# Logits between projections and scores: another order on TensorE and VectorE in a fused attention and soft-mixture kernel

## The chip, the core and the metric

The kernel runs on one core of a Trainium2 chip. The metric is the device time of one execution in microseconds, from a program that computes everything in a single launch.

## The reference

For x of shape 16 x 256 x 128 (4096 tokens of width 128), layer-normalised to xn, three things are added up:

```python
out = x + attention(xn) + soft_moe(xn)
# attention: 2 x 16 heads of width 64, causal, o = softmax(q1 k1) v1 - lam * softmax(q2 k2) v2, then o @ Wo
# soft_moe:
logits = (xn @ phi_w.T + phi_b).reshape(t, z, 64, 32)     # 64 experts x 32 slots = 2048 columns
D = softmax(logits, axis=3)                               # over an expert's 32 slots: "dispatch"
C = softmax(logits, axis=2)                               # over the 64 experts: "combine"
X_tilde = einsum('tznp,tzd->npd', D, xn)                  # then clip, layernorm, tanh
Y = einsum('tznp,npH->tzH', C, X_tilde @ expert_w + expert_b)
```

Everything is in 32-bit floats. Most products are made of three matmuls (`product3`) from high and low halves of the operands.

## The kernel before

The kernel has three phases: setup (layer norm, transposes of xn), a main phase and a combine phase. The change is in the main phase alone.

The main phase walks through 128 steps, written as `for it in range(ITER + 2): for j in range(4): step(it, j, ...)`, with `ITER` = 32. A step v = 4 it + j does two things side by side.

* Attention for one sequence and four heads: two sequences of one group of heads are a unit, and a unit takes two steps. In odd steps (j of 1 or 3) TensorE makes the queries and keys of the next unit (`project`, four groups of three matmuls). In even steps it makes the values (`make_v`) and multiplies an earlier unit's output by Wo (`times_wo`). In each step it transposes the probabilities of step v-2 (`transposes`), makes the scores of v (`scores`) and the attention output of v-2 (`output`).
* The mixture for a quarter j (512 columns) of the logits of token tile `it`: `logits` in this step, `dispatch` for the tile before.

There are eight groups of heads, each 16 steps long. At each of the seven edges between them, weights are split into halves: ScalarE copies the new projections' high half in the last iteration's step j = 1 (`projections_high`), VectorE makes the low half in j = 2, the low halves of the value weights in j = 3 (`values_low`, ahead of the score maxima), and that of Wo in j = 3 of the next iteration (`output_low`).

Each engine has one queue and works through it in the order in which the steps write it; semaphores join the engines. The order in a step is:

* TensorE (`step`, L656): transposes, projections or (values, Wo), scores, outputs, logits, dispatch.
* VectorE (`step`, L923): `inverse` of the row sums of step v-1, then `dispatch_sum`, query copies, `dispatch_inverse`, a running maximum `slot_max`; in even steps instead the low half of `o_t` and the emptying of Wo; the score maxima `bank_max`; the column maximum `slot_max_end` and inverse (j = 0) or the column sum `slot_sum` (j = 3); `take_logits`, `take_slots`, `group_max`.
* ScalarE: in even steps the high half of `o_t` (L755), which waits for its turn behind the exponentials of the step before, then copies of the transposed probabilities, values or keys, two exponentials of the mixture, and the eight exponentials of the scores (L731).
* GpSimd: subtract the group maximum, multiply the attention probabilities by the inverse (L1043, L1045), add banks, multiply dispatch, subtract the column maximum.

PSUM has eight banks. `take_bank` makes TensorE wait until the last user of a bank has been emptied:

```python
BANKS = {0: ps_tu[:, 0, :], 1: ps_tu[:, 1, :], "t0": ps_t[:, 0, :], "t1": ps_t[:, 1, :], "s2": ps_s[:, 2, :]}
P_BANK = (0, 1, "t0", "t1")      # projections
V_BANK = (0, 1)                  # values
T_BANK = ("t0", "t1", "s2")      # transposes
WO_BANK, LG_BANK = "t0", 0       # Wo, logits
```

SyncE copies the slice `fx` of the next tile's transposed tokens (L469) once the dispatch of the tile before is done; `logits` waits for it.

Of the kernel before, what the change touches and what calls it, by code (L numbers as in the profile page):

```python
# [34 lines left out]
NTT = NT // P  # L35
# [30 lines left out]
def live(i, n):  # L66

    return 0 <= i < n
# [279 lines left out]
def main_phase(nc, env):  # L348

    with ExitStack() as ctx:  # L350
# [60 lines left out]
        P_BANK = (0, 1, "t0", "t1")  # L411
        V_BANK = (0, 1)
        T_BANK = ("t0", "t1", "s2")
        WO_BANK, LG_BANK = "t0", 0
        c_stored = [[sem(f"c_stored{r}{j}") for j in range(4)] for r in range(2)]
        SB = (1, 2, 0)

# [8 lines left out]
        def bank_of(buf, t, j):  # L426

            return buf[:, (t % 2) * NS_ + j * BK:(t % 2) * NS_ + (j + 1) * BK]
# [4 lines left out]
        def back(it, j, n):  # L433

            return it + (j - n) // 4, (j - n) % 4
# [98 lines left out]
        def _(pe):  # L534
            last_use = {}

            def take_bank(b, by, count):

                if b in last_use:
                    wait(pe, *last_use[b])  # L540
                last_use[b] = (by, count)
                return BANKS[b]
# [48 lines left out]

            def logits(t, j):
                pe.wait_ge(fx_in, 32 * (t + 1))
                out = take_bank(LG_BANK, lg_out, 4 * t + j + 1)
                product3(pe, out, fx[0][:], fx[1][:], phiT[0][:, j * BK:(j + 1) * BK],
                         phiT[1][:, j * BK:(j + 1) * BK]).then_inc(lg_mm, 1)

# [49 lines left out]
            def times_wo(unit, g, b):  # L647

                pe.wait_ge(env["wo_hi"], g + 1)
                pe.wait_ge(env["wo_lo"], g + 1)  # L650
                pe.wait_ge(o_hi, unit + 1)
                pe.wait_ge(o_lo, unit + 1)
                out = take_bank(b, wo_out, unit + 1)
                product3(pe, out, wo_w[0][:], wo_w[1][:], o_t[0][:], o_t[1][:]).then_inc(wo_mm, 1)

            def step(it, j, g, kk):  # L656
                v = 4 * it + j
                unit = 2 * it + j // 2
                if live(v - 2, NV):
                    for k in range(3):  # L660
                        transposes(v - 2, j % 2, k)
                if j % 2 == 1:
                    if live(unit + 1, NU):
                        for i in range(G):
                            project(unit + 1, (j // 2 + 1) % 2, g + 1 if (kk, j) == (PER - 1, 3) else g, i, P_BANK[i])
                else:
                    if live(unit, NU):
                        for half in range(2):
                            make_v(unit, (j // 2) % 2, g, half, V_BANK[half])
                    if live(unit - 2, NU) and v != NV + 2:  # L670
                        times_wo(unit - 2, g - 1 if kk == 0 else g, WO_BANK)
                if live(v, NV):
                    scores(v, j, unit)
                if v == NV + 1:
                    dispatch(LAST, 1)
                if live(v - 2, NV):
                    output(v - 2, (j + 2) % 4, unit - 1)
                if live(it, NTT):
                    logits(it, j)
                if live(it - 1, NTT) and v != NV + 1:  # L680
                    dispatch(it - 1, j)

# [131 lines left out]
        def _(dve):  # L814
# [20 lines left out]
            def next_queries(it, j, i):  # L835
                unit = 2 * it + j // 2 + 1
                if live(unit, NU):
                    take_queries(unit, (j // 2 + 1) % 2, i, P_BANK[i])
# [8 lines left out]
            def inverse(v, q):  # L847
                if live(v, NV):
                    dve.wait_ge(exp_done, 3 * v + 3)
                    wait(dve, norm_done, v - 1)  # L850
                    nc.vector.reciprocal(inv[:, q, :], total[:, q, :]).then_inc(inv_done, 1)

            def take_logits(t, j):
                if t == 0 and j == 0:
                    dve.wait_ge(bias_in, 16)
                dve.wait_ge(lg_mm, 4 * t + j + 1)
                if t >= 2:

                    dve.wait_ge(c_bank, 3 * (t - 2) + max(j, 1))
                    dve.wait_ge(c_stored[t % 2][j], 16 * (t // 2))  # L860
                nc.vector.tensor_tensor(bank_of(logit, t, j), BANKS[LG_BANK],  # L861
                                        bias[:, j * BK:(j + 1) * BK], ALU.add).then_inc(lg_out, 1)

            def group_max(t, j):
# [6 lines left out]
            def slot_max(t, j):  # L871
                if live(t, NTT) and j > 0:

                    wait(dve, m_bank, 3 * t + j - 1)
                    wait(dve, m_done, t)
                    before = bank_of(logit, t, 0) if j == 1 else m_run[:]
                    nc.vector.tensor_tensor(m_run[:], before, bank_of(logit, t, j), ALU.max).then_inc(m_bank, 1)

            def slot_max_end(t):
                if live(t, NTT):  # L880
                    dve.wait_ge(m_bank, 3 * (t + 1))
                    wait(dve, m_done, t)
                    nc.vector.tensor_reduce(m_all[:, t % 2 * NP_:(t % 2 + 1) * NP_],
                                            m_run[:].rearrange("p (e s) -> p s e", s=NP_), AX.X,
                                            ALU.max).then_inc(m_done, 1)

            def dispatch_sum(t, j):
                if live(t, NTT):
                    dve.wait_ge(d_exp, 4 * t + j + 1)
                    nc.vector.tensor_reduce(dsum[:, j, :], by_expert(bank_of(disp, t, j)), AX.X,  # L890
                                            ALU.add).then_inc(d_sum, 1)

            def dispatch_inverse(t, j):
                if live(t, NTT):
                    n = 4 * t + j
                    dve.wait_ge(d_sum, n + 1)
                    wait(dve, d_norm, n - 3)
                    nc.vector.reciprocal(dinv[:, j, :], dsum[:, j, :]).then_inc(d_inv, 1)

            def slot_sum(t):  # L900
                if live(t, NTT):

                    dve.wait_ge(c_bank, 3 * (t + 1))
                    wait(dve, c_sum, t)
                    nc.vector.tensor_reduce(c_all[:, t * NP_:(t + 1) * NP_],
                                            by_expert(c_run[:]).rearrange("p e s -> p s e"), AX.X,
                                            ALU.add).then_inc(c_sum, 1)
# [15 lines left out]
            def step(it, j, g, kk):  # L923
                v = 4 * it + j
                unit = 2 * it + j // 2
                inverse(v - 1, (j + 1) % 2)
                if j % 2 == 1:
                    dispatch_sum(*back(it, j, 2))
                    next_queries(it, j, 0)
                    dispatch_inverse(*back(it, j, 2))  # L930
                    next_queries(it, j, 1)
                    slot_max(*back(it, j, 1))
                    if live(g + 1, NG) and (kk, j) == (PER - 1, 3):
                        values_low(nc, dve, env, g + 1)
                    if live(g, NG) and (kk, j) == (0, 3) and g > 0:
                        output_low(nc, dve, env, g)
                else:
                    if live(unit - 2, NU):

                        dve.wait_ge(o_hi, unit - 1)  # L940
                        nc.vector.tensor_tensor(o_t[1][:], ps_o[:, 0, :], f32(o_t[0][:]), ALU.subtract
                                                ).then_inc(o_lo, 1)
                    dispatch_sum(*back(it, j, 2))
                    dispatch_inverse(*back(it, j, 2))
                    slot_max(*back(it, j, 1))
                    if live(unit - 2, NU) and v != NV + 2:
                        take_wo(unit - 2, WO_BANK)
                if live(v, NV):
                    bank_max(v, j)
                if live(g + 1, NG) and (kk, j) == (PER - 1, 2):  # L950
                    projections_low(nc, dve, env, g + 1)
                if j == 0:
                    slot_max_end(it - 1)
                if j == 3:
                    if it < ITER:
                        slot_sum(it - 2)
                if j == 0 and it < ITER + 1:
                    slot_inverse(it - 3)
                if live(it, NTT):
                    take_logits(it, j)  # L960
                take_slots(it - 1, j)
                if live(it, NTT):
                    group_max(it, j)
# [376 lines left out]
```

## Time and profile before

| | |
|---|---|
| runs (3) | median 1325.7 us, 1323.85 to 1325.83 |
| profiled execution | 1325.38 us, its span 1323.5 us |
| mean granted TensorE clock | 0.989 |
| instructions | 29570 |
| DMA | 126.31 MB, mean 95 GB/s |

The span is the time from the first to the last instruction; the profiled execution's own time has 1.9 us around it. Times inside the trace are counted from the span's start. An engine is busy while one of its instructions runs; matmuls are pipelined, so their shown durations overlap, and the distance between the starts of two groups says what a group takes.

### The profile page before, as it was taken

To read this page: it belongs to the slowest core of one execution; us is meant where nothing else is said; L and a number is where in the kernel's file an instruction comes from. 1 tells how busy PE (TensorE), PEld (TensorE's weight loads), DVE (VectorE), ACT (ScalarE), POOL (GpSimd) and SP (SyncE) were. 2 spreads that over 40 slices of the span, in tenths; PEclk is the share of its full clock that TensorE was granted. 3 is DMA by queue.
4 is the path that set the end of the run, shared out by engine and by line. 5 is a ranking of instruction groups with operands and counts; after the bars stand their busy time and mean duration, and the time that the engine had idled before them with its cause. 6 is when DMAs were issued, how large, how long until landed. Compare 5 with 4: busy or idle time off the path is not lost. (4 is left out here: it accounts for less than half of the span.)

```text
span 1323.5 us, 29570 instructions
## 1 busy us (share of the span) xinstructions
PE 1263.7 (95%) x9136; PEld 991.8 (75%) x9136; DVE 1157.0 (87%) x3633; ACT 1062.8 (80%) x3218; POOL 1096.2 (83%) x847
## 2 busy tenths in 40 slices
PE   2999999999999999999999999999999999689998
PEld 2777777777777777777777777777777777478887
DVE  7688999889988998899889988998899988878876
ACT  4688988888888888888888888888898888655554
POOL 1478888888888888888888888888888888789985
PEclk9899999999999999999999999999999999889999
DMA  5111122112111221112211211122111117547783
GB/s 172 54 53 68 71 83 73 71 71 74 58 70 71 76 77 66 70 71 83 73 71 71 72 60 71 69 79 73 68 66 71 71 71 209 154 156 252 250 264 118
DMA packets 105980, 126.31 MB, mean 95 GB/s; under 512 B 20192, under 2 KB 56032, under 8 KB 105696
## 3 DMA queue, kind: packets, MB, share of 16 engines
q1 hardware_dynamic: 102160, 122.97, 27.7%
q10 hardware_dynamic: 3664, 1.44, 0.5%
q8 instruction: 75, 1.23, 0.4%
q14 instruction: 81, 0.66, 0.2%
HBM read 48.89 MB, written 35.65 MB: 64 GB/s over the span
## 5 line engine op out<-in xcount | busy, mean ns | idle before, releaser
L731 ACT ACTIVATE e<-e,neg_max 128x256 f32<-128x256 f32 (+1 forms) x1024 | 451.4, 442 | 58.0 <-DVE neg_max L826 57.3
L826 DVE CUSTOM_DVE_ANT_0 e<-ps_s,mask 128x256 f32<-128x256 f32 (+1 forms) x1024 | 294.1, 351 | 68.0 <-PE ps_s L573 68.0
L1037 POOL TENSOR_TENSOR disp<-logit,gmax 128x512 f32<-128x512 f32 x128 | 134.4, 1050 | 192.5 <-DVE gmax L868 192.5
L1045 POOL TENSOR_TENSOR e<-e,inv 128x1024 f32<-128x1024 f32 x128 | 285.7, 2232 | 0.0
L573 PEld LDWEIGHTS ps_s<-qk 64*128 64x128 f32 x2048 | 172.9, 186 | 49.7 <-issue 45.1
L573 PE MATMUL ps_s<-qk 64*128 64x256 f32 (+1 forms) x2048 | 203.2, 337 | 0.0
L731 ACT ACTIVATION_READ_ACCUMULATOR e<-e,neg_max 128x1 f32 x1024 | 191.2, 187 | 0.0
L556 PEld LDWEIGHTS ps_t<-ident,e 128*128 128x128 f32 x1024 | 119.9, 141 | 68.1 <-issue 64.9
L1073 POOL TENSOR_TENSOR logit<-logit,m_all 128x512 f32<-128x512 f32 x128 | 165.0, 1290 | 0.0
L745 ACT ACTIVATE qk<-ps_t 128x512 f32<-128x512 f32 x126 | 75.3, 598 | 83.8 <-PE ps_t L80 78.7
L617 PE MATMUL ps_o<-pT,v_sb 128*64 128x256 f32 x1024 | 138.8, 392 | 0.0
L717 ACT ACTIVATE pT<-ps_t 128x512 f32<-128x512 f32 x256 | 135.9, 581 | 3.1 <-PE ps_t L556 3.1
L1064 POOL TENSOR_TENSOR disp<-disp,dinv 128x512 f32<-128x512 f32 x128 | 137.4, 1073 | 0.0
L1222 ACT ACTIVATE c_hi<-ps_c 128x512 fp32r<-128x512 f32 x128 | 76.8, 600 | 71.6 <-PE ps_c L1196 71.6
L556 PE MATMUL ps_t<-ident,e 128*128 128x128 f32 x1024 | 132.8, 273 | 1.1 <-POOL e L1045 1.0
L1043 POOL TENSOR_TENSOR e<-e,inv 128x512 f32<-128x512 f32 x128 | 133.6, 1044 | 0.0
L603 PE MATMUL ps_tu<-disp,fxn 128*128 128x512 f32 x256 | 130.7, 593 | 0.0
L861 DVE TENSOR_TENSOR logit<-ps_tu,bias 128x512 f32<-128x512 f32 x128 | 86.3, 674 | 30.1 <-PE ps_tu L80 27.7
L1248 DVE TENSOR_TENSOR c_lo<-ps_c,c_hi 128x512 fp32r<-128x512 f32 x128 | 86.9, 687 | 29.1 <-ACT c_hi L1222 28.6
L845 DVE TENSOR_TENSOR xt_acc<-ps_tu,xt_acc 128x512 f32<-128x512 f32 x128 | 87.7, 686 | 10.5 <-PE ps_tu L603 10.1
L617 PEld LDWEIGHTS ps_o<-pT,v_sb 128*64 128x64 f32 x1024 | 62.1, 136 | 36.4 <-ACT pT L717 0.8
L832 DVE TENSOR_SCALAR qk<-ps_tu 128x512 f32<-128x512 f32 x128 | 84.3, 659 | 5.1 <-PE ps_tu L80 3.3
(162 smaller groups left out, 3267.2 us busy)
## 6 DMA issues: line engine op xcount, KB each, us to landing
xs<-xT SPq DMA_DIRECT2D x128, 256.0 KB, 2.4
c_scratch<-logit SPq DMA_DIRECT2D x128, 256.0 KB, 2.1
xT<-c_scratch SPq DMA_DIRECT2D x16, 1024.0 KB, 5.4
disp<-c_scratch SPq DMA_DIRECT2D x8, 1024.0 KB, 5.5
logit<-c_scratch SPq DMA_DIRECT2D x8, 1024.0 KB, 6.8
fx<-xT SPq DMA_DIRECT2D x64, 64.0 KB, 1.9
fxn<-xn SPq DMA_DIRECT2D x32, 64.0 KB, 1.9
xT<-in_L_ffn_expert_w SPq DMA_DIRECT2D x4, 512.0 KB, 6.7
```

Of the source, the lines that this page charges most:

```text
L556: mm = pe.transpose(bank[:, i * P:(i + 1) * P], src, ident[:])
L573: return pe.matmul(out, queries, keys, start=(i, tile) in ((0, 1), (1, 0), (1, 1)), stop=True, skip_group_check=True)
L603: pe.matmul(out, fxn[:], bank_of(disp, t, j), start=True, stop=True).then_inc(xt_mm, 1)
L617: mm = pe.matmul(ps_o[rows, 0, b * S:(b + 1) * S], v_sb[q][:, 2 * b, cols], pT[:, part, (i % 2) * S:(i % 2 + 1) * S], start=(b == 0 and pa ...
L717: nc.scalar.activation(pT[:, k, :], BANKS[T_BANK[k]], ACT.Copy).then_inc(t_out, 1)
L731: ins = nc.scalar.activation(dst, dst, ACT.Exp, bias=neg_max[:, q, c:c + 1], scale=-1.0, accum_out=total[:, q, c:c + 1])
L826: nc.vector.tensor_tensor_reduce(out=dst, in0=part, in1=here, scale=-1.0, scalar=HIGHEST, op0=ALU.add, op1=ALU.min, accum_out=neg_max[:, q ...
L1037: nc.gpsimd.tensor_tensor(by_expert(bank_of(disp, t, jj)), by_expert(bank_of(logit, t, jj)), gmax[:, jj, :].unsqueeze(2).to_broadcast([P, ...
L1043: nc.gpsimd.tensor_tensor(e0[q][:], e0[q][:], inv[:, q, 0:G].unsqueeze(2) .to_broadcast([P, G, P]), ALU.mult)
L1045: nc.gpsimd.tensor_tensor(e1[q][:], e1[q][:], inv[:, q, G:2 * G].unsqueeze(2) .to_broadcast([P, G, S]), ALU.mult).then_inc(norm_done, 1)
L1064: nc.gpsimd.tensor_tensor(bank, bank, dinv[:, jj, :].unsqueeze(2).to_broadcast([P, EB, NP_]), ALU.mult).then_inc(d_norm, 1)
L1073: nc.gpsimd.tensor_tensor(bank, bank, m_all[:, t % 2 * NP_:(t % 2 + 1) * NP_].unsqueeze(1) .to_broadcast([P, EB, NP_]), ALU.subtract).then ...
```

## The change

Three things are done. The logits are issued ahead of the scores, so that they follow the projections or Wo, and those of even j go into PSUM bank t1 instead of bank 0. VectorE makes the attention inverse later in its step, behind `dispatch_sum` and the first query copy (odd steps) or behind `o_t` and `dispatch_sum` (even steps). And the column maximum and its inverse (moved from j = 0 to j = 1) and the column sum (j = 3) are issued ahead of the score maxima instead of behind them.

```diff
-        WO_BANK, LG_BANK = "t0", 0
+        WO_BANK, LG_BANK = "t0", ("t1", 0)
...
-                out = take_bank(LG_BANK, lg_out, 4 * t + j + 1)
+                out = take_bank(LG_BANK[j % 2], lg_out, 4 * t + j + 1)
...
+                if live(it, NTT):
+                    logits(it, j)
                 if live(v, NV):
                     scores(v, j, unit)
                 if v == NV + 1:
                     dispatch(LAST, 1)
                 if live(v - 2, NV):
                     output(v - 2, (j + 2) % 4, unit - 1)
-                if live(it, NTT):
-                    logits(it, j)
                 if live(it - 1, NTT) and v != NV + 1:
                     dispatch(it - 1, j)
...
-                nc.vector.tensor_tensor(bank_of(logit, t, j), BANKS[LG_BANK],
+                nc.vector.tensor_tensor(bank_of(logit, t, j), BANKS[LG_BANK[j % 2]],
...
-                inverse(v - 1, (j + 1) % 2)
                 if j % 2 == 1:
                     dispatch_sum(*back(it, j, 2))
                     next_queries(it, j, 0)
+                    inverse(v - 1, (j + 1) % 2)
                     dispatch_inverse(*back(it, j, 2))
                     next_queries(it, j, 1)
                     slot_max(*back(it, j, 1))
+                    if j == 1:
+                        slot_max_end(it - 1)
+                        if it < ITER + 1:
+                            slot_inverse(it - 3)
+                    elif it < ITER:
+                        slot_sum(it - 2)
...
                     dispatch_sum(*back(it, j, 2))
+                    inverse(v - 1, (j + 1) % 2)
                     dispatch_inverse(*back(it, j, 2))
...
-                if j == 0:
-                    slot_max_end(it - 1)
-                if j == 3:
-                    if it < ITER:
-                        slot_sum(it - 2)
-                if j == 0 and it < ITER + 1:
-                    slot_inverse(it - 3)
```

## Rows read from the trace of the kernel before

**Rows 1.** The page's busy table: us, share of the span, instructions.

```profile
PE 1263.7 (95%) x9136; PEld 991.8 (75%) x9136; DVE 1157.0 (87%) x3633; ACT 1062.8 (80%) x3218; POOL 1096.2 (83%) x847
```

**Rows 2.** TensorE's time line over two ordinary steps (start, us, engine, line, operation).

```profile
510.34 1.58 PE L573 MATMUL ps_s<-qk 64*128 64x256 f32 x16
...
513.30 0.50 PE L78 MATMUL ps_tu<-phiT,fx 128*128 128x512 f32 x1
...
514.10 1.02 PE L603 MATMUL ps_tu<-disp,fxn 128*128 128x512 f32 x2
514.96 1.04 PE L556 MATMUL ps_t<-ident,e 128*128 128x128 f32 x8
...
517.70 0.40 PE L78 MATMUL ps_t<-o_t,wo_w 128*128 128x512 f32 x1
...
518.50 1.58 PE L573 MATMUL ps_s<-qk 64*128 64x256 f32 x16
...
527.25 1.58 PE L573 MATMUL ps_s<-qk 64*128 64x256 f32 x16
```

**Rows 3.** The wait table, 150 to 1080 us: total us, times, longest.

```profile
PE ps_tu L78 <- DVE logit L861: 6.6, 7, 1.3
PE ps_t L78 <- DVE o_t L941: 4.2, 14, 0.3
```

**Rows 4.** Time line of VectorE and ScalarE in the odd step of rows 2.

```profile
511.50 0.42 DVE L826 CUSTOM_DVE_ANT_0 e<-ps_s,mask 128x256 f32<-128x256 f32 x1 [1.11 <-PE ps_s L573]
...
513.73 1.09 DVE L905 TENSOR_REDUCE c_all<-c_run 128x32 f32<-128x512 f32 x1
...
514.73 0.69 DVE L861 TENSOR_TENSOR logit<-ps_tu,bias 128x512 f32<-128x512 f32 x1
...
515.58 0.57 ACT L755 ACTIVATE o_t<-ps_o 128x512 fp32r<-128x512 f32 x1
```

**Rows 5.** Time line of an early step in which Wo waits for o_t.

```profile
68.77 0.57 ACT L755 ACTIVATE o_t<-ps_o 128x512 fp32r<-128x512 f32 x1
...
69.37 0.69 DVE L941 TENSOR_TENSOR o_t<-ps_o,o_t 128x512 fp32r<-128x512 f32 x1 [0.28 <-ACT o_t L755]
...
70.32 0.47 PE L78 MATMUL ps_t<-o_t,wo_w 128*128 128x512 f32 x1
...
71.19 1.15 PE L573 MATMUL ps_s<-qk 64*128 64x256 f32 x10
```

**Rows 6.** The page's table of DMA issues: KB each, us from issue to landing.

```profile
fx<-xT SPq DMA_DIRECT2D x64, 64.0 KB, 1.9
```

**Rows 7.** Time lines at the first edge between weight groups.

```profile
152.85 0.61 ACT L118 ACTIVATE a_w<-a_raw 128x512 fp32r<-128x512 f32 x1
...
155.78 1.58 PE L573 MATMUL ps_s<-qk 64*128 64x256 f32 x16
...
164.06 2.35 POOL L1045 TENSOR_TENSOR e<-e,inv 128x1024 f32<-128x1024 f32 x1
...
164.57 1.98 DVE L139 SCALAR_TENSOR_TENSOR v_w<-v_raw,v_w 128x128 fp32r<-128x128 f32 x1
...
166.47 1.13 DVE L139 SCALAR_TENSOR_TENSOR v_w<-v_raw,neg_lam,v_w 128x128 fp32r<-128x128 f32 x1
...
174.36 1.58 PE L573 MATMUL ps_s<-qk 64*128 64x256 f32 x16
```

**Rows 8.** Wo's low half in setup and in the loop, and scores around it.

```profile
33.17 0.29 DVE L152 TENSOR_TENSOR wo_w<-wo_raw,wo_w 128x128 fp32r<-128x128 f32 x1
...
191.31 1.58 PE L573 MATMUL ps_s<-qk 64*128 64x256 f32 x16
...
200.04 1.98 DVE L152 TENSOR_TENSOR wo_w<-wo_raw,wo_w 128x128 fp32r<-128x128 f32 x1
...
208.78 1.58 PE L573 MATMUL ps_s<-qk 64*128 64x256 f32 x16
```

## The prediction

> **What bounds the kernel now.** I read the busy table first: TensorE 95%, GpSimd 83% of 1323.5 us [rows 1]. Nobody is clearly free, so the question is which wait ends last. TensorE's time line answers it [rows 2]. In an odd step (j of 1 or 3) the scores start at 510.34, the logits 2.96 later, dispatch 0.80 after them, the transposes 0.86 after that, Wo at 517.70 and the next scores at 518.50: 8.16 us, each group starting where the one before ends. The even step takes 8.75 us (518.50 to 527.25). TensorE bounds the main phase, at 16.91 us for a pair of steps. The wait table says how little it waits for others: 6.6 us in 7 waits for bank 0 (logits not yet emptied, values want it) and 4.2 us in 14 waits for o_t in front of Wo [rows 3]. So the change can win little, and must be read for what it makes late.
>
> Next in line is the exponent path of an odd step. VectorE's first score maximum comes 1.16 us after the scores (511.50); ScalarE is through its eight exponentials and at the copy of o_t 4.08 us after that (515.58) [rows 4]. From that copy to Wo it is 1.55 us where Wo really waits for it: copy at 68.77, VectorE's low half at 69.37 (idle until ScalarE), Wo at 70.32; and from there 0.87 us to the next scores instead of 0.80 [rows 5]. Added up, Wo can start 1.16 + 4.08 + 1.55 = 6.79 us after the odd scores. TensorE gets there after 7.36 us (517.70 less 510.34). The path has 0.57 us to spare, if VectorE is free for o_t.
>
> **Part 1: logits ahead of the scores.** Nothing is removed: 128 groups of three matmuls stay. A group costs 0.80 us now, of which 0.10 is entry: its first matmul shows 0.50 us, where Wo's, of the same size behind its own kind, shows 0.40 [rows 2]. In the new place it stands behind its own kind: 0.70. Dispatch now follows the outputs directly, a pair that the trace has not. Bounds: 0 (dispatch behind logits has no gap) and 0.10 (logits behind the same outputs) [rows 2]. I take 0.10, the row with the same predecessor. By the Trainium skill, "TensorEngine Tiling (Array Packing)", Key Properties, a change of tiling mode drains TensorE, which speaks for the 0.10 too, the outputs being 64-row tiles; no run here shows the pair alone.
>
> What matters more: the logits leave the stretch from scores to Wo, so TensorE is at Wo 7.36 - 0.70 = 6.66 us after the scores (6.56 with a free entry of dispatch), while the exponent path still takes 6.79. Wo becomes the late one. The odd-to-even leg is 6.79 + 0.87 + 0.70 (logits) = 8.36 in place of 8.16, **+0.20**, whatever dispatch's entry costs. The other leg has no Wo, and ScalarE idles there before its keys: 8.75, or 8.65 with the free entry. VectorE is in time: its maxima take 2.23 us (511.50 to 513.73) [rows 4], so it empties the logits from 3.4 to 4.1 us after the scores, slots and group maxima reach to 5.4, and o_t's copy ends at 5.8.
>
> **Part 2: bank t1 for even logits.** The next transposes start 2.96 + 0.10 + 0.86 = 3.92 after the scores and want t1 for their second four, about 0.43 later (half of what eight take): 4.35. The emptying ends at 4.1, and a signal takes 0.1 to 0.2: in time by a hair. Odd logits stay in bank 0, so the 6.6 us of waits, which lie at the edges of part 4, are not removed. By the Trainium skill, "Perfetto Trace Analysis", Matmuls, independent groups should rotate through PSUM banks; by that alone the kernel would win up to those 6.6 us.
>
> SyncE copies the next tile's fx behind dispatch. Dispatch ends at 514.96 [rows 2] and a copy lands 1.9 us after its issue [rows 6], near 517.5 for the second; the logits that need it now come where the scores stood, at 518.5: hidden, 1 us to spare.
>
> **Part 3: VectorE's order.** The inverse goes behind dispatch_sum and the first query copy (odd), or behind o_t and dispatch_sum (even); so 0.7 to 1.4 us later against the group maximum, and GpSimd's two multiplies wait for it. In an even step it is ready about 7.3 us after the odd scores (5.8, then two instructions of 0.7); the multiplies take some 3.4 (the longer 2.35 [rows 7]) and end at 10.8, the transposes that need them start at 8.36 + 3.92 = 12.3. Hidden; without that cover each late inverse would cost its own 0.7. The column maximum with its small inverse (j = 1) and the column sum (j = 3; 1.0 us, 513.73 to 514.73) go ahead of the odd score maxima, where VectorE idles 1.11 now [rows 4], and 1.8 behind part 1: hidden. What queues behind them are these maxima, and behind those the whole exponent path; at 1.8 the cover ends.
>
> **Part 4: the edges of the seven weight groups**, where the covers are gone.
> (a) The odd step with ScalarE's copy of the new projections, 0.61 us (0.53 to the next start), ahead of o_t [rows 7]: 6.79 + 0.53 + 0.87 + 0.70 = 8.89 for 8.17. **+0.72**, seven times 5.0.
> (b) The odd step with VectorE's two low halves of the value weights ahead of the maxima. They run from 164.57 to 167.60, and the pair of steps takes 18.58 us (155.78 to 174.36) [rows 7]. The column sum now pushes them by 1.0. But they are short work: such an instruction takes 0.29 us at the kernel's start and 1.98 in the loop [rows 8], and the first of them ends 0.14 after GpSimd's multiply (164.06 for 2.35) [rows 7]. So GpSimd sets their end, and it begins about 0.35 later (the later inverse). I take 0.4: maxima 12.15 us after the even scores, for 11.75. From first maximum to next scores it is 4.08 + 1.55 + 0.87 + 0.70 = 7.20, so 19.35 for 18.58: **+0.75** rounded, 5.3. A wait of 0.6 for t1 in that even step goes under in it. By the Trainium skill, "SBUF — State Buffer", SBUF: two separate sides, a VectorE instruction with two SBUF inputs and a GpSimd one shut each other out for a whole instruction; the rows agree. Without it the full column sum would count: 1.33 each, 9.3.
> (c) The odd step with the low half of Wo, 1.98 us, in that place: GpSimd's multiplies end about 7.05 + 3.4 = 10.4 after the even scores, the maxima start at 10.5, and 10.5 + 7.20 = 17.7 stands for 17.47 (191.31 to 208.78) [rows 8]. **+0.25**, 1.8; at full price 0.87, 6.1.
>
> **The end.** The last maxima too stand behind a column sum, with all the rest of the phase behind them: +1.0.
>
> **Sum.** Of 64 pairs 21 are edges and two lie at the ends; 41 at +0.20 give 8.2. With 5.0, 5.3, 1.8 and 1.0 that is 21.3, on the profiled execution's 1325.4 us (span 1323.5, 1.9 around it): 1346.7, **1347**; the median of the runs stands 0.3 above that execution. With the free entry 62 even legs give back 0.10: 1340.5. With the column sums at full price it is 8.3 more: 1355.
>
> **Rivals.**
> *Faster: the exponent path fits.* If Wo is ready within TensorE's 6.66 us, no ordinary leg grows; with the free entry 128 steps save 0.10, 12.8 us, and if the edges are sheltered as well: 1313. It decides at 0.13 us of the exponent path (0.23 with the free entry). Against it: 4.08 and 1.55 are direct rows.
> *No change:* the same, with the edges at their price (12) and the end: 1325.
> *Edges only:* ordinary legs unchanged, entry 0.10: 1338.
> *Bank t1 or GpSimd binds.* The room at t1 is thin: VectorE 0.3 late in each even step gives 62 waits of 0.2 with a restart, 15 to 20 us: 1365. For it: GpSimd is 83% busy and starts later.
>
> **Chances.** Forecast (1338 to 1355) 0.66; edges only 0.12; t1 or GpSimd 0.10; faster 0.07; no change 0.05. The range, 1331 to 1359, leaves out the faster and the unchanged case and most of t1. A measurement of this kernel tells about 0.2% (2.7 us) from nothing. Faster 0.07, same 0.05, slower 0.88.
>
> **What would show it.** Right: Wo idle until VectorE's o_t in nearly all even steps, 6.8 after the odd scores; that leg near 8.36, at edge (a) 8.9, the pair at edge (b) near 19.3. Wrong: Wo closed up at 6.66 or less; transposes waiting for logits in t1; the value halves pushed by the whole column sum; dispatch with no entry cost.

## The result and the profile after

The changed kernel takes 1347.6 us (median of 4 runs, 1346.9 to 1349.2) against 1325.6 us: 1.0175 times as long, 95% interval 1.0162 to 1.0187. Its profiled execution has a span of 1346.2 us, 22.7 more. (A leg, below, is the time from the scores of one step to those of the next; a pair is an even and an odd step together.)

The page's busy table of the changed kernel:

```profile
PE 1276.6 (95%) x9136; PEld 992.1 (74%) x9136; DVE 1132.2 (84%) x3633; ACT 1062.1 (79%) x3218; POOL 1099.5 (82%) x847
```

Beside [rows 1] nothing looks worse. TensorE still shows 95%, and VectorE is even 25 us less busy. A busy table can't show this loss; the distances between starts can. TensorE's time line over two ordinary steps:

```profile
519.73 1.58 PE L573 MATMUL ps_s<-qk 64*128 64x256 f32 x16
...
522.69 1.12 PE L603 MATMUL ps_tu<-disp,fxn 128*128 128x512 f32 x2
523.65 1.04 PE L556 MATMUL ps_t<-ident,e 128*128 128x128 f32 x8
...
526.53 0.47 PE L78 MATMUL ps_t<-o_t,wo_w 128*128 128x512 f32 x1
...
527.30 0.40 PE L78 MATMUL ps_t<-phiT,fx 128*128 128x512 f32 x1
...
528.09 1.58 PE L573 MATMUL ps_s<-qk 64*128 64x256 f32 x16
...
531.05 1.12 PE L603 MATMUL ps_tu<-disp,fxn 128*128 128x512 f32 x2
532.01 1.15 PE L556 MATMUL ps_t<-ident,e 128*128 128x128 f32 x8
...
536.96 1.36 PE L573 MATMUL ps_s<-qk 64*128 64x256 f32 x12
```

Against [rows 2]: the odd-to-even leg is 8.36 us (519.73 to 528.09) for 8.16. Wo starts 6.80 after the odd scores, earlier than before (7.36), but TensorE was through with the values at about 6.66. Wo's first matmul shows 0.47 us for 0.40 and the logits behind it 0.40 for 0.50, as forecast. The transposes start 0.96 behind dispatch, for 0.86: dispatch has taken the logits' entry of 0.10. The other leg (528.09 to 536.96) is 8.87, and that is not the 8.75 that was forecast.

The exponent path in the odd step, from VectorE's time line and then from ScalarE's:

```profile
519.48 1.07 DVE L905 TENSOR_REDUCE c_all<-c_run 128x32 f32<-128x512 f32 x1
...
520.89 0.42 DVE L826 CUSTOM_DVE_ANT_0 e<-ps_s,mask 128x256 f32<-128x256 f32 x1 [0.34 <-PE ps_s L573]
...
525.58 0.69 DVE L947 TENSOR_TENSOR o_t<-ps_o,o_t 128x512 fp32r<-128x512 f32 x1 [0.44 <-ACT o_t L755]
```

```profile
524.97 0.58 ACT L755 ACTIVATE o_t<-ps_o 128x512 fp32r<-128x512 f32 x1
```

First maximum 1.16 behind the scores, o_t's copy 4.08 behind the maximum, Wo 1.56 behind the copy: the terms of [rows 4, 5]. VectorE now waits for ScalarE in front of o_t. The column sum lies in the idle time ahead of the maxima, of which 0.34 is left.

From the wait table, 150 to 1100 us (total us, times, longest):

```profile
POOL e L1043 <- DVE inv L851: 59.4, 100, 1.6
...
DVE o_t L947 <- ACT o_t L755: 29.8, 54, 1.2
...
PE ps_t L78 <- ACT pT L717: 13.3, 22, 0.9
...
PE ps_tu L78 <- DVE logit L861: 2.5, 7, 0.4
PE ps_t L556 <- DVE logit L861: 1.9, 7, 0.3
```

New are GpSimd's 59.4 us for the late inverse; VectorE's wait for o_t has grown from 1.3 to 29.8. The third row names ScalarE's copy of probabilities as what Wo waits for. By the code only the first of these copies concerns Wo (bank t0), and it is over some 0.5 us earlier; experiment e3 decides between it and o_t. The single starts speak for o_t: in 62 of the 64 units Wo starts 0.26 us behind the end of VectorE's low half, in the kernel before in 17. The waits for bank 0 fell from 6.6 to 2.5 [rows 3].

At the first edge, VectorE and then GpSimd:

```profile
167.52 1.06 DVE L905 TENSOR_REDUCE c_all<-c_run 128x32 f32<-128x512 f32 x1
...
168.50 0.99 DVE L139 SCALAR_TENSOR_TENSOR v_w<-v_raw,v_w 128x128 fp32r<-128x128 f32 x1
...
169.42 1.13 DVE L139 SCALAR_TENSOR_TENSOR v_w<-v_raw,neg_lam,v_w 128x128 fp32r<-128x128 f32 x1
```

```profile
167.01 2.34 POOL L1045 TENSOR_TENSOR e<-e,inv 128x1024 f32<-128x1024 f32 x1
...
169.31 1.09 POOL L1064 TENSOR_TENSOR disp<-disp,dinv 128x512 f32<-128x512 f32 x1
```

The first half starts later than before and takes 0.99 us where [rows 7] show 1.98. It ends 0.14 after GpSimd's multiply (169.49 and 169.35), the second 0.15 after the next (170.55 and 170.40), just as before.

Adding up between the scores of step 4 and those of step 126: 1069.7 us (72.17 to 1141.86) for 1048.5 (71.19 to 1119.67), 21.2 more. The other 1.5 lie ahead of step 4 (1.0) and behind step 126 (0.5).

### The profile page after: what moved, and what is told of

Same layout as the page of the kernel before. It is cut to its first block and busy times, and to the rows that moved or that the text cites. A ratio compares the mean times of both kernels' runs of the same rounds, so it can differ in the third digit from the quotient of the medians.

```text
span 1346.2 us, 29569 instructions
## 1 busy us (share of the span) xinstructions
PE 1276.6 (95%) x9136; PEld 992.1 (74%) x9136; DVE 1132.2 (84%) x3633; ACT 1062.1 (79%) x3218; POOL 1099.5 (82%) x847
## 5 line engine op out<-in xcount | busy, mean ns | idle before, releaser
L1045 POOL TENSOR_TENSOR e<-e,inv 128x1024 f32<-128x1024 f32 x128 | 255.9, 1999 | 0.0
L1043 POOL TENSOR_TENSOR e<-e,inv 128x512 f32<-128x512 f32 x128 | 165.2, 1291 | 71.4 <-DVE inv L851 69.9
L603 PE MATMUL ps_tu<-disp,fxn 128*128 128x512 f32 x256 | 143.7, 644 | 0.0
L556 PE MATMUL ps_t<-ident,e 128*128 128x128 f32 x1024 | 138.4, 275 | 4.9 <-DVE logit L861 3.6
L868 DVE TENSOR_REDUCE gmax<-logit 128x16 f32<-128x512 f32 x128 | 86.4, 675 | 0.1
```

Source lines behind the costliest of these rows:

```text
L556: mm = pe.transpose(bank[:, i * P:(i + 1) * P], src, ident[:])
L603: pe.matmul(out, fxn[:], bank_of(disp, t, j), start=True, stop=True).then_inc(xt_mm, 1)
L1043: nc.gpsimd.tensor_tensor(e0[q][:], e0[q][:], inv[:, q, 0:G].unsqueeze(2) .to_broadcast([P, G, P]), ALU.mult)
L1045: nc.gpsimd.tensor_tensor(e1[q][:], e1[q][:], inv[:, q, G:2 * G].unsqueeze(2) .to_broadcast([P, G, S]), ALU.mult).then_inc(norm_done, 1)
```

## The experiments

All ratios are to the kernel before, on the same chip.

**e1: VectorE's new order alone.** Against the changed kernel:

```diff
-        WO_BANK, LG_BANK = "t0", ("t1", 0)
+        WO_BANK, LG_BANK = "t0", (0, 0)
...
-                if live(it, NTT):
-                    logits(it, j)
                 if live(v, NV):
                     scores(v, j, unit)
...
                     output(v - 2, (j + 2) % 4, unit - 1)
+                if live(it, NTT):
+                    logits(it, j)
```

> The kernel before with the change's VectorE order alone (late inverse; column maximum, its inverse and the column sum ahead of the odd score maxima); logits stay behind the outputs in bank 0. Exponent-path theory: TensorE still reaches Wo 7.36 us after the odd scores, the path needs 6.79, and the moved reductions fit in VectorE's 1.1 to 1.4 us of idle time ahead of the odd maxima. So ordinary pairs stay at 16.91 us and the time stays at 1326, 1322 to 1330. Rival (the moved reductions or the late inverse are themselves the loss): 1335 or more, with pairs above 17.0.

Measured 1328.1 us, ratio 1.0016 (1.0007 to 1.0025). TensorE's time line of an odd step:

```profile
511.55 1.58 PE L573 MATMUL ps_s<-qk 64*128 64x256 f32 x16
...
518.91 0.40 PE L78 MATMUL ps_t<-o_t,wo_w 128*128 128x512 f32 x1
...
519.71 0.49 PE L573 MATMUL ps_s<-qk 64*128 64x256 f32 x3
```

Wo at 7.36 and 8.16 us to the next scores, as before. What it loses is at the edges: (b) takes 18.95 us for 18.58 and (c) 17.6 for 17.47; the ordinary pairs stay at 16.92. So the moved reductions and the late inverse are not by themselves what costs in the changed kernel.

**e2: TensorE's new order alone.** The kernel before with

```diff
-        WO_BANK, LG_BANK = "t0", 0
+        WO_BANK, LG_BANK = "t0", ("t1", 0)
...
+                if live(it, NTT):
+                    logits(it, j)
                 if live(v, NV):
                     scores(v, j, unit)
...
-                if live(it, NTT):
-                    logits(it, j)
```

> The kernel before with logits ahead of the scores and even logits in t1, VectorE's order untouched. Exponent-path theory: the leg from odd to even scores grows as in the changed kernel, and the reductions behind the maxima now hold up the emptying of t1 (j = 0, about 1.3 us of reductions, so transposes wait about 1.15 us, 31 times) and, in j = 3, push o_t behind the group maximum by about 0.6 us: 1385 to 1400, far above the changed kernel. Rival (the two halves of the change are independent, the TensorE order carries the whole loss): 1347.

Measured 1383.9 us, ratio 1.0446 (1.0431 to 1.0461); a little below the range forecast. VectorE and then TensorE in a step with j = 0, whose scores started at 544.62:

```profile
548.02 1.07 DVE L883 TENSOR_REDUCE m_all<-m_run 128x32 f32<-128x512 f32 x1
549.00 0.34 DVE L914 RECIPROCAL c_all<-c_all 128x32 f32<-128x32 f32 x1
549.26 0.63 DVE L861 TENSOR_TENSOR logit<-ps_t,bias 128x512 f32<-128x512 f32 x1
```

```profile
549.94 0.66 PE L556 MATMUL ps_t<-ident,e 128*128 128x128 f32 x4 [0.80 <-DVE logit L861]
```

The two reductions hold up the emptying of t1, and the transposes wait for it. The leg is 9.78 us. In j = 3 the column sum behind the maxima pushes o_t too: that leg is 8.7 us in nearly all ordinary steps, for 8.36 in the changed kernel (5 us over sixteen of them). In the new TensorE order VectorE's new order is worth 36 us, without it it costs 2.5. The two halves of the change are not independent.

**e3: o_t's high copy early.** The changed kernel; ScalarE copies the outputs behind its sixth exponential of the odd step (`copy_output` holds the two waits and the copy that stood in the even step):

```diff
+                        if (k, i) == (0, 2) and j % 2 == 1:
+                            copy_output((v + 1) // 2 - 2)
                         done += 1
                         act.wait_ge(max_done, done)
...
-                if j % 2 == 0:
-                    if live(unit - 2, NU):
-
-                        act.wait_ge(av_mm, 2 * (unit - 1))
-                        wait(act, wo_mm, unit - 2)
-                        nc.scalar.activation(o_t[0][:], ps_o[:, 0, :], ACT.Copy).then_inc(o_hi, 1)
+                if v >= NV + 2 and j % 2 == 0:
+                    copy_output(unit - 2)
```

> The changed kernel with ScalarE's high copy of o_t made in the odd step, behind the sixth of its eight exponentials, instead of behind all eight in the even step. Same work, the copied probabilities come at the same time as now. Exponent-path theory: Wo no longer waits for o_t, it starts 6.7 us after the odd scores, the odd-to-even leg goes back to about 8.15 and edge (a) loses its extra 0.5: 1326 to 1331. Rival (Wo waits for bank t0, that is for ScalarE's copy of the transposed probabilities, which the trace names as releaser in 22 waits): Wo stays at 6.8 and the time at 1347.

Measured 1330.1 us, ratio 1.0037 (1.0025 to 1.0048). ScalarE and then TensorE, odd step:

```profile
516.91 0.57 ACT L723 ACTIVATE o_t<-ps_o 128x512 fp32r<-128x512 f32 x1
...
517.77 0.39 ACT L739 ACTIVATE e<-e,neg_max 128x128 f32<-128x128 f32 x1
...
518.16 1.06 ACT L717 ACTIVATE pT<-ps_t 128x512 f32<-128x512 f32 x2
```

```profile
512.44 1.58 PE L573 MATMUL ps_s<-qk 64*128 64x256 f32 x16
...
519.11 0.40 PE L78 MATMUL ps_t<-o_t,wo_w 128*128 128x512 f32 x1
...
519.81 0.39 PE L78 MATMUL ps_t<-phiT,fx 128*128 128x512 f32 x1
...
520.60 0.70 PE L573 MATMUL ps_s<-qk 64*128 64x256 f32 x5
```

Wo starts 6.67 us after the scores, in one piece with the values (0.40, no entry), and the leg is 8.16. The probabilities are copied at 5.72 after the scores, as late as in the changed kernel (5.71). So Wo waited for o_t, and the releaser in the wait table was the wrong name. One edit to one engine's order takes back 17.5 of 22 us. Edge (a) falls from 8.89 to 8.52, not to 8.16. There the other candidate is the late one: at the first such edge ScalarE's first copy of the probabilities (bank t0), which stands behind its copy of the new projections, ends at 155.27 and Wo starts 0.14 us later, while o_t's low half has been over for 0.95.

**e4: the inverse first.** The changed kernel with `inverse(v - 1, (j + 1) % 2)` again at the head of VectorE's step.

> The changed kernel with the attention inverse back at the head of VectorE's step. Theory that the late inverse makes GpSimd late, so that the first add of banks ends after VectorE wants to overwrite that logits bank in j = 0 and the transposes wait 0.12 us for t1: the wait goes, about 31 times 0.12 and 0.2 at each edge (b), 1342 to 1344. Rival (the lateness in j = 0 has another source; the inverse is hidden, as the prediction had it): 1347 to 1348.

Measured 1343.0 us, ratio 1.0140 (1.0123 to 1.0156). The missing piece of the even leg is this. In the changed kernel, GpSimd and then VectorE behind the even scores of 528.09:

```profile
527.05 1.54 POOL L1043 TENSOR_TENSOR e<-e,inv 128x512 f32<-128x512 f32 x1 [0.79 <-DVE inv L851]
528.55 1.89 POOL L1045 TENSOR_TENSOR e<-e,inv 128x1024 f32<-128x1024 f32 x1
530.40 1.26 POOL L1055 TENSOR_TENSOR c_run<-logit 128x512 f32<-128x512 f32 x1
```

```profile
531.76 0.69 DVE L861 TENSOR_TENSOR logit<-ps_t,bias 128x512 f32<-128x512 f32 x1 [0.19 <-issue]
```

In j = 0, `take_logits` overwrites the bank that GpSimd's first add (L1055) reads and waits for it. GpSimd waited 0.79 us for the inverse, the add ends at 531.66, the emptying of t1 starts at 531.76 with 0.19 us idle before it, 3.67 after the scores and not at 3.4, and the transposes lose 0.12. It is so in every step with j = 0 from 8 to 124: the emptying starts 0.09 behind the add, 3.66 to 3.68 after the scores. In e4 it starts at 3.39 in all but one, and the leg is 8.76 (527.11 to 535.87):

```profile
527.11 1.58 PE L573 MATMUL ps_s<-qk 64*128 64x256 f32 x16
...
535.87 1.36 PE L573 MATMUL ps_s<-qk 64*128 64x256 f32 x13
```

Edge (c) falls from 17.59 to 17.12, edge (b) rises from 19.13 to 19.50. At the first edge (b), VectorE and then TensorE:

```profile
157.97 2.08 DVE L877 TENSOR_TENSOR m_run<-logit 128x512 f32<-128x512 f32 x1
```

```profile
164.63 0.66 PE L556 MATMUL ps_t<-ident,e 128*128 128x128 f32 x4 [1.11 <-DVE logit L861]
```

VectorE's running maximum starts while GpSimd's multiply runs (157.61 to 159.50) and shows 2.08 us, for 0.63 in the changed kernel (157.50). The maxima, the low half of the projections and the emptying of t1 come late behind it, and the transposes wait 1.11 us instead of 0.26. So the time lies in the forecast range for other reasons than forecast: between steps 4 and 126 the steps with j = 0 give back 2.9 us and edge (c) 3.1, edge (b) takes 2.3 more, and another 2.8 come from behind step 126, where nothing was forecast (0.6 are lost ahead of step 4; the two profiled executions are 5.8 us apart).

**e5: all logits in bank 0.** The changed kernel with `LG_BANK` = (0, 0).

> The changed kernel with all logits in bank 0 (t1 not used for them). Bank 0 then holds the first half of the values when the even logits come; ScalarE empties it behind o_t's copy and three copies of probabilities, some 0.25 us after the logits would start. Theory: the even logits wait about 0.3 us with a restart 62 times, while the 0.12 us waits for t1 vanish: 1359 to 1366. Rival (the bank of the logits is immaterial in this order): 1344 to 1348.

Measured 1374.4 us, ratio 1.0369 (1.0355 to 1.0383). The direction was right, the size too small:

```profile
558.81 0.47 PE L78 MATMUL ps_t<-o_t,wo_w 128*128 128x512 f32 x1
...
559.90 0.47 PE L78 MATMUL ps_tu<-phiT,fx 128*128 128x512 f32 x1 [0.16 <-ACT v_sb L739]
...
560.76 1.58 PE L573 MATMUL ps_s<-qk 64*128 64x256 f32 x15
```

The logits start 1.09 behind Wo instead of 0.77 and need an entry again: an ordinary odd-to-even leg takes 8.74, 0.38 more, and I had put 0.3. With the edges (0.96 at each edge (b)) these legs cost 27.8 us; the waits for t1 in j = 0 vanish, as expected, and give back 3.6. Of the rest 5.1 us lie ahead of step 4, and their cause is open. In this order the second bank is needed, and it is right to have it.

**e6: the early copy in the kernel before.**

> The kernel before with the early high copy of o_t. Exponent-path theory: this path has 0.57 us to spare in ordinary steps and at edges (b) and (c) it is VectorE, not ScalarE, that comes late to o_t, so nothing is gained: 1324 to 1327, ordinary pairs 16.91. Rival (the path costs in the kernel before too, so the early copy helps whatever the order): 1320 or less, by the 4.2 us of waits for o_t.

Measured 1324.6 us, ratio 0.9997 (0.9988 to 1.0006): nothing. The same edit gives 17.5 us in the new order and none in the old, where the path had 0.57 us to spare.

**e8 and e9: the edges repaired as well.** Both orders with the early copy, o_t's low half ahead of the inverse and the inverse ahead of `dispatch_sum` (so e9 also takes back the changed kernel's late inverse), and

```diff
-                    if live(g + 1, NG) and (kk, j) == (PER - 1, 3):
-                        values_low(nc, dve, env, g + 1)
-                    if live(g, NG) and (kk, j) == (0, 3) and g > 0:
-                        output_low(nc, dve, env, g)
...
+                if live(g + 1, NG) and (kk, j) == (PER - 1, 3):
+                    values_low(nc, dve, env, g + 1)
+                if live(g, NG) and (kk, j) == (0, 3) and g > 0:
+                    output_low(nc, dve, env, g)
                 if live(it, NTT):
                     take_logits(it, j)
```

> The kernel before with the early copy, o_t's low half ahead of the inverse, and the low halves of the value and Wo weights between the column sum and the emptying of the logits, where GpSimd is idle and waits for the group maximum. Theory that these short VectorE instructions are long only because they wait for GpSimd's running multiply: they show 0.3 us instead of 1 to 2, the maxima are no longer late, edge (b) falls from 18.58 to about 17.2 and edge (c) from 17.47 to about 16.95: 1312 to 1316. Rival (they are slow in themselves in the loop, whatever runs on GpSimd): 1.98 us stays and the values wait for bank 0 as long as before: 1322 to 1326.

> The changed kernel with the same three repairs as e8. Exponent-path theory: TensorE's work is the same in both orders (0.10 of entry moved from logits to dispatch), so with the path shortened the pairs are 16.92 and what is left against e8 is the wait for t1 behind the low half of the projections, about 0.5 to 0.8 at seven edges, plus 1 to 2 at both ends: 1317 to 1323. Rival (the new order has a cost of its own): pairs stay above 17.0 and the time above 1330.

e8 takes 1311.1 us, ratio 0.9892 (0.9879 to 0.9906), the fastest version here. e9 takes 1316.8, ratio 0.9937 (0.9924 to 0.9951). The groups of these instructions in the kernel before (us in total, mean ns), and then in e8:

```profile
L152 DVE TENSOR_TENSOR wo_w<-wo_raw,wo_w 128x128 fp32r<-128x128 f32 x8 | 14.2, 1771 | 0.0
L139 DVE SCALAR_TENSOR_TENSOR v_w<-v_raw,v_w 128x128 fp32r<-128x128 f32 x8 | 14.1, 1764 | 0.0
L139 DVE SCALAR_TENSOR_TENSOR v_w<-v_raw,neg_lam,v_w 128x128 fp32r<-128x128 f32 x8 | 8.3, 1034 | 0.0
```

```profile
L139 DVE SCALAR_TENSOR_TENSOR v_w<-v_raw,neg_lam,v_w 128x128 fp32r<-128x128 f32 x8 | 2.8, 349 | 0.0
L152 DVE TENSOR_TENSOR wo_w<-wo_raw,wo_w 128x128 fp32r<-128x128 f32 x8 | 2.3, 285 | 0.0
L139 DVE SCALAR_TENSOR_TENSOR v_w<-v_raw,v_w 128x128 fp32r<-128x128 f32 x8 | 2.3, 285 | 0.0
```

GpSimd and then VectorE at the first edge (b) of e8:

```profile
166.09 1.30 POOL L1078 TENSOR_TENSOR logit<-logit,m_all 128x512 f32<-128x512 f32 x1
```

```profile
167.63 0.29 DVE L139 SCALAR_TENSOR_TENSOR v_w<-v_raw,v_w 128x128 fp32r<-128x128 f32 x1
```

The same instructions, the same data: 36.6 us become 7.4 where GpSimd is idle. Edge (b) is 17.21 in e8, edge (c) 16.94. In e9 the ordinary pairs are 16.92, so TensorE's new order has no cost of its own in ordinary steps once the path is short and the inverse early. What remains against e8 between steps 4 and 126, 5.5 us, is at the edges, half and half: 2.8 at edge (a), where the leg stays at 8.52 as in e3 (8.16 in e8), and 2.7 at edge (b), with the t1 wait behind the projections' low half (even leg 9.23 at the first edge, 10.19 at the third).

**e10 and e11: this last edit alone**, in the changed kernel and in the kernel before.

> The changed kernel with only the low halves of the value and Wo weights moved between the column reductions and the emptying of the logits. Theory (edges (b) and (c) cost because these halves wait for GpSimd ahead of the maxima): they take 0.3 us there, edge (b) falls from 19.14 to about 17.6 and edge (c) from 17.6 to about 17.15; ordinary pairs keep their 17.13 to 17.24, edge (a) its 8.9: 1332 to 1336. Rival (the ordinary pairs grow only as an echo of the edges): they fall back to 16.9 too, 1322.

> The kernel before with only the low halves moved. Same theory: nearly all of e8's gain comes from this one edit, since the exponent path has room in the old order: 1311 to 1315. Rival (e8 needed the early copy of o_t): 1318 or more.

e10: 1335.3 us, ratio 1.0088 (1.0071 to 1.0105); edges (b) 17.71 and (c) 17.11 (one of seven 17.74), ordinary pairs 17.13 to 17.24 as in the changed kernel. The ordinary pairs are no echo of the edges. e11: 1312.9 us, ratio 0.9917 (0.9902 to 0.9933): most of e8's gain is this edit.

## Why the prediction was right, and where it was not

*What bounds the kernel.* Right. TensorE's groups stay closed except where named waits open them.

*Part 1, logits ahead of the scores.* Right to a few hundredths: Wo at 6.80 (6.79 forecast), leg 8.36 (8.36), dispatch's entry 0.10 (the value taken, not the free one). The rule of the Trainium skill quoted there ("TensorEngine Tiling (Array Packing)", Key Properties) leads one to expect it, and the tiling does change: the outputs are 128*64 tiles in the trace (64 columns; "64-row" in the prediction is a slip), dispatch is 128*128. But the cause of the 0.10 is not separated here. An entry of 0.09 also shows where the tiling stays 128*128, from the transposes to the projections: their first two matmuls start 0.32 apart (533.35 and 533.67), the next two 0.23. The legs of the 40 ordinary pairs add up to 8.3. That o_t is the link is shown by e3 and, from the other side, by e6. (In the sum I wrote that "62 even legs" would give back the free entry; meant were the legs from even to odd scores.)

*Part 2, bank t1.* "In time by a hair" was right for ordinary steps with j = 2 (8.77) and wrong for j = 0. The waits for bank 0 at the edges, 6.6 us, were to stay and fell to 2.5. The column sum no longer stands ahead of the emptying; but e1, which has that too, still shows 4.6, and what takes off the rest is not separated.

*Part 3, "hidden in an even step".* This step failed. I followed the late inverse to the transposes, where it is hidden, and not to GpSimd's later instructions. Its first add frees a logits bank, VectorE waits for that, and TensorE for VectorE: 0.11 us in each of 31 steps with j = 0, 3.4 us. e4 shows it. The moved reductions are hidden in ordinary steps, as said (e1).

*Part 4, the edges.* (a) 8.89 for 8.17, +0.72 as forecast; 4.9 over the seven. (b) 19.13 for 18.58 at the first edge, +0.55; over the seven 3.5 where 5.3 was forecast (one of them took 19.03 before). The maxima start 11.94 after the even scores (11.75 before, 12.15 forecast): GpSimd's multiply starts 8.48 after them for 8.28, so 0.20 later and not 0.35. The wait for t1 in that even step makes it 9.23 long (0.46 over an ordinary one; 0.6 was written). (c) 17.59 for 17.47, +0.12 for 0.25: 0.9 for 1.8; the maxima start at 10.42 (10.5 forecast, 10.63 before). The shelter by GpSimd was right in kind and larger than taken; at the full price of the column sum the forecast had 15.4 for the two.

*The sum.* Over the steps 4 to 126 the two traces differ by 21.2 us: 8.3 in the legs of the ordinary pairs with Wo, 4.9 at (a), 3.5 at (b), 0.9 at (c), 3.4 in the steps with j = 0, 0.2 elsewhere. The forecast for this stretch was 20.3: it lacked the 3.4 and had (b) and (c) 2.8 too high. That the total comes out so well is in part luck. The 1.0 ahead of step 4 (not forecast) and the 0.5 behind step 126 (1.0 forecast) are not shown to come from the change: with TensorE's old order the scores of step 4 start anywhere from 69.90 (e8) to 72.16 (e11), and what follows step 126 takes 203.8 to 205.2 us.

## What to carry to other kernels

When a bound engine's groups are closed up, moving one group costs next to nothing there (here 0.10 us of entry went from the logits to dispatch); what it does is shorten the time that some other chain had. Work out that chain from the same starting point for both orders (here 6.79 against 7.36 and 6.66) before counting anything else. Follow a delayed instruction to every consumer of every later instruction on its engine, not only to its own. And a short instruction with a long duration is worth a look at what runs on the neighbour at that moment: moving three of them gave about 12 us (e11), more than any order of the large ones tried here.

## What was not expected of the hardware

The wait table named ScalarE's copy (22 waits, 13.3 us), and these waits are for VectorE's o_t. In all 22 the last of the two copies in that row ends 0.02 to 0.03 us before Wo, o_t's low half 0.26 before it, so the nearer event was named though Wo doesn't depend on it. With o_t early (e3) 8 such waits are left, 4.3 us. There the first copy ends 0.14 before Wo and o_t's low half 0.57 or more, and the name is right.

That a half of 128x128 is short (0.29 us) wherever GpSimd is idle had been argued from two rows. The means say it: 1.77, 1.76 and 1.03 us before against 0.29, 0.29 and 0.35 in e8, e9 and e11. And so does every single one of these instructions in the traces of before, the changed kernel and e8 to e11: each that starts while a GpSimd instruction runs ends 0.14 to 0.16 us after that instruction's end, and each of the others takes 0.28 to 0.36. In e10 two of the three kinds still run into the end of a GpSimd subtraction and show 0.58 to 0.60.
